# Two passages of a three-stage graph kernel: weights on another queue, columns reloaded in pieces, a pipelined split, and no barrier before the attention

## The reference, cut to what matters

```python
deg = maximum(segment_sum(1, dst), 1);  norm = deg ** -0.5
h = maximum(layernorm(x), 0)
for W_r, W_sl, W_el in (layer 1, layer 2):                 # "messages"
    own = where(in_degree == 0, h @ W_el, h @ W_sl)
    agg = segment_sum((rel_embed[type] + h[src]) @ W_r, dst)
    h = rrelu(agg * norm + own)
x = x + h
h = maximum(layernorm(x), 0)                               # "attention"
qk = h @ Wqk + bqk;  v = h @ Wv + bv
scores = clip(sum(qk[dst] * qk[src], -1) / sqrt(128), -5, 5)
out = segment_sum(softmax over each dst (scores) * v[src], dst) @ Wo + bo
x = x + layernorm(h + out) * gamma + beta
```

## Time and profile before

| | before |
|---|---|
| median of 3 runs | 870.51 us (868.87 to 872.46) |
| the profiled execution's own time | 870.01 us |
| its span, first to last instruction | 868.3 us |
| TensorE busy | 732.6 us, 84% |
| VectorE / ScalarE / GpSimd busy | 61% / 50% / 28% |
| mean granted clock of TensorE | 0.944 of full speed |
| stages by TensorE | counting and layer one to 372.7, passage to 431.2, layer two to 562.4, passage to 573.8, attention to the end |

### The profile page before, as it was taken

How to read it: one execution, slowest core, us unless ns; L and a number is a source line. 1 busy time by engine, 2 the same in 40 slices (tenths; PEclk the granted TensorE clock), 3 DMA queues, 4 the chain that set the end, 5 groups by cost and what they waited for, 6 DMA issues and landing times. The chain is left out here.

```text
span 868.3 us, 15380 instructions
## 1 busy us (share of the span) xinstructions
PE 732.6 (84%) x5767; PEld 545.2 (63%) x5767; DVE 527.7 (61%) x931; ACT 431.5 (50%) x1085; POOL 245.1 (28%) x273
## 2 busy tenths in 40 slices
PE   4266698898889898977399999859999999999993
PEld 3255587788778788866289999824444444444463
DVE  4987997786768677541033333414476767666676
ACT  0445765564555555551011111237767676767661
POOL 6130010000001111100000000026666666666662
PEclk9999799799989999987699999979999999999996
DMA  4100200033300000011311111130000000000000
GB/s 130 33 1 18 59 2 7 23 103 71 100 9 7 8 8 7 8 60 61 108 31 37 36 37 37 37 106 1 1 4 21 3 22 2 24 0 24 2 25 18
DMA packets 39763, 27.89 MB, mean 32 GB/s; under 512 B 5311, under 2 KB 38163, under 8 KB 39686
## 3 DMA queue, kind: packets, MB, share of 16 engines
q1 hardware_dynamic: 39206, 26.35, 10.5%
q10 hardware_dynamic: 480, 0.53, 0.2%
HBM read 13.28 MB, written 10.80 MB: 28 GB/s over the span
## 5 line engine op out<-in xcount | busy, mean ns | idle before, releaser
L1462 POOL TENSOR_TENSOR counts<-counts,work 125x500 f32<-125x500 f32 x150 | 162.3, 1082 | 97.5 <-DVE work L1526 84.1
L1016 PE MATMUL sums<-work 125*128 125x196 f16 (+15 forms) x1220 | 157.1, 256 | 24.7 <-DVE work L825 24.6
L1384 PE MATMUL a_ps_o<-work 125*128 125x500 f32 (+1 forms) x350 | 159.2, 545 | 7.1 <-DVE work L1530 6.7
L1526 DVE SCALAR_TENSOR_TENSOR work<-a_ps_s,counts 125x500 f32<-125x500 f32 x150 | 101.6, 677 | 93.5 <-ACT a_ps_s L1482 93.4
L1372 PE MATMUL a_ps_s<-work 128*125 128x500 f32 x300 | 152.0, 589 | 6.9 <-PEq L534 6.9
L819 DVE TENSOR_TENSOR work<-work,counts 125x3024 f16<-125x3024 f16 (+1 forms) x60 | 114.3, 1906 | 65.5 <-PE sums L1018 62.4
L1477 ACT ACTIVATE a_ps_s<-a_ps_s,work 125x500 f32<-125x500 f32 (+1 forms) x157 | 102.1, 650 | 86.5 <-PE a_ps_s L1372 83.4
L1018 PE MATMUL sums<-work 125*128 125x10 f16 (+15 forms) x800 | 133.7, 196 | 0.0
L1187 ACT CAST counts<-sums 128x364 f32 (+38 forms) x305 | 131.9, 472 | 2.1 <-issue 1.4
L977 PE MATMUL sums<-counts 125*128 125x250 f16 (+1 forms) x975 | 124.5, 275 | 10.0 <-ACT work L1129 10.0
L825 DVE TENSOR_TENSOR work<-work,counts 125x4200 f16<-125x4200 f16 (+15 forms) x120 | 125.5, 1086 | 0.0
(11 more groups left out here) (178 smaller groups left out, 703.3 us busy)
## 6 DMA issues: line engine op xcount, KB each, us to landing
first_columns<-counts SPq DMA_DIRECT2D x5, 610.4 KB
counts<-first_columns SPq DMA_DIRECT2D x5, 610.4 KB
counts<-counts SPq DMA_DIRECT2D x5, 468.8 KB
counts<-in_x SPq DMA_DIRECT2D x5, 312.5 KB
h_nodes<-counts SPq DMA_DIRECT2D x5, 312.5 KB
work<-in_x SPq DMA_DIRECT2D x12, 125.0 KB
x_after_messages<-work SPq DMA_DIRECT2D x12, 125.0 KB
h_attention<-work SPq DMA_DIRECT2D x12, 125.0 KB
```

The source lines that it names most:

```text
L1016: pe.matmul(win[:, 0:c, cols], lo[:, k * 2 * LO:k * 2 * LO + 128], m[:, k, h0 * w:(h0 + c) * w].rearrange("p (h d) -> p h d", d=w), start= ...
L1384: last = pe.matmul(ps_o[c % 2][:, 0:cols(u) // n], h3[:, j + i, :], pbuf[u % PB][:, i * NP:i * NP + cols(u) // n], start=j + i == 0, stop= ...
L1462: pool.tensor_tensor(a, a, p, ALU.add).then_inc(acc_done, 1)
L1526: dve.scalar_tensor_tensor(pbuf[u % PB], ps_s[u % 4][0:NP, 0:WIDE], float(np.exp(-CLIP)), counts[0:NP, j, c * WIDE:(c + 1) * WIDE], ALU.ma ...
```

## The change

Five edits. (1) Layer two's weights and the last chunk's x are issued by ScalarE, after its last split piece. (2) The five DMAs of `first_columns` are issued by SP one per chunk, behind the h3 store of the first five chunks of layer two. (3) h of layer one comes back from the moment at which all batches but the last are free. (4) Between the layers TensorE's steps stand in an order written out; chunk 11 uses other PSUM banks (2 and 3) and another buffer for the turned h; the split is pipelined over pieces on ScalarE and VectorE, and ten source blocks of layer two's first sum stand ahead of agg of chunk 12. (5) The two blocks of engine programs become one: each engine goes from the messages to the attention by itself, the first three scores, two clips, one exponent and one product stand before the last chunk is turned, and that turn and its qk stand inside units 1 and 3.

```diff
 @block.sync
-            sp.wait_ge(ring_free, len(BATCHES))
+            sp.wait_ge(ring_free, len(BATCHES) - 1)
             sp.wait_ge(h1_out, 16 * DIRECT)
...
-            sp.wait_ge(sums_done, CHUNKS)
-            for i in range(5):
-                v = slice(5 * i, 5 * i + 5)
-                sp.dma_start(counts[0:NP, v, 0:HEAD], heads.rearrange("p (j d) -> p j d", d=HEAD)[:, v, :]).then_inc(heads_in, 16)
...
-            for t, v in zip((wr, ws[:, 0:D], ws[:, D:]), weights2):
-                sp.dma_start(t, v).then_inc(L["wts"], 16)
-            sp.dma_start(wqk, wqk_d).then_inc(L["wts"], 16)
-            sp.dma_start(bqk, bqk_d.rearrange("(p o) -> p o", o=1)).then_inc(L["wts"], 16)
-            sp.dma_start(x_last, by_block(x, LAST)).then_inc(L["last_in"], 16)
...
                 sp.dma_start(h3[:, c * LB * D:(c + 1) * LB * D], xc.rearrange("p b f -> p (b f)")).then_inc(L["h3_out"], 16)
+                if i < 5:
+                    v = slice(5 * i, 5 * i + 5)
+                    sp.dma_start(counts[0:NP, v, 0:HEAD], heads.rearrange("p (j d) -> p j d", d=HEAD)[:, v, :]).then_inc(heads_in, 16)
...
             sp.wait_ge(L["x2_last"], 16)
+            sp.wait_ge(L["rows"], CHUNKS)
+            A["sync"](sp)
 @block.vector
             ending(DIRECT)
+            split(0, 0)
             for i in range(4):
-                split(i)
-            split(4)
+                split(i + 1, 0)
+                split(i, 1)
+            split(4, 1)
             ending(DIRECT + 1)
...
                 dve.tensor_scalar(mv2[:, 0:nb, 1], mv2[:, 0:nb, 1], EPS, None, ALU.add).then_inc(L["var"], 1)
+                if i == LAST:
+                    A["vector_first"](dve)
                 dve.wait_ge(L["root"], i + 1)
 @block.tensor
-                    pe.wait_ge(put, 2 * READY[c])
+                    pe.wait_ge(put, 2 * READY[c] if c <= DIRECT else 2 * GROUPS)
...
+            for kind, c in (("own", DIRECT + 1), ("agg", DIRECT), ("sum", DIRECT + 1), ("self", DIRECT + 1),
+                            ("rest", DIRECT + 1), ("own", LAST), ("agg", DIRECT + 1), ("sum", LAST), ("self", LAST), ("rest", LAST)):
+                for step in by_kind.pop((kind, c)):
+                    layer1(*step)
+            own(0, ORDER2[0])
+            sums(0, ORDER2[0], 0, EARLY).then_inc(early, 1)
+            layer1("agg", LAST, 0)
...
-            h3_turn(LAST, ORDER2[LAST])
-            qk(LAST, ORDER2[LAST])
+            pe.wait_ge(L["rows"], LAST)
+            A["tensor_first"](pe)
+            A["tensor"](pe, last_turn, last_qk)
 @block.scalar
+            layer1("own", DIRECT + 1)
+            split(0, 0)
+            for i in range(4):
+                split(i + 1, 0)
+                split(i, 1)
+            split(4, 1)
+            layer1("self", DIRECT + 1)
+            layer1("rest", DIRECT + 1)
+            layer1("own", LAST)
+            split(5, 0)
+            split(5, 1)
+            layer1("self", LAST)
+            layer1("rest", LAST)
+            split(6, 0)
+            split(6, 1)
...
+            act.wait_ge(agg_done, CHUNKS)
+            for t, v in zip((wr, ws[:, 0:D], ws[:, D:]), weights2):
+                act.dma_start(t, v).then_inc(L["wts"], 16)
+            act.dma_start(wqk, wqk_d).then_inc(L["wts"], 16)
+            act.dma_start(bqk, bqk_d.rearrange("(p o) -> p o", o=1)).then_inc(L["wts"], 16)
+            act.dma_start(x_last, by_block(x, LAST)).then_inc(L["last_in"], 16)
...
+            A["scalar_first"](act)
             act.wait_ge(L["x2_ready"], CHUNKS)
             act.dma_start(by_block(x2, LAST), tmp[:, 0:1, :]).then_inc(L["x2_last"], 16)
...
+            A["scalar"](act, last_turned, last_rows)
 def attention
-    with nc.Block() as block:
+    def scalar_first(act):
+        act.wait_ge(consts, 2)
+        below(act, 0)
+        below(act, 1)
+        exponent(act, 0)
+
+    def run_scalar(act, last_turned, last_rows):
+        for u, (c, j, n) in enumerate(units):
+            if 0 < u < len(units) - 1:
+                below(act, u + 1)
+            if u:
+                exponent(act, u)
+            if u == 1:
+                last_turned()
+            if u == 3:
+                last_rows()
```

More of the change, by code:

```diff
@@ L326, in messages @@
     hn_in = [sem(f"hn_in{i}") for i in range(4)]
-    rounded2, parts2_ready = sem("rounded2"), sem("parts2_ready")
+    rounded2, parts2_ready = ([sem(f"{n}{i}") for i in range(2)] for n in ("rounded2_", "parts2_ready"))
+    early = sem("early")
     slots, at_slot = plan()
@@ L458, in again_dve @@
     def again_dve(dve):
+        dve.wait_ge(early, 1)
         dve.memset(zeros_r, 0.0).then_inc(R["begin"], 1)
@@ L528, in messages @@
                                      "h3_t_out", "qk", "power")}
+    L["rows"] = T["rows"]
     LAST = CHUNKS - 1
@@ L1034, in _ @@
                         pe.reg_load(flag, T["flag"][0:1, 0:1])
-            for step in slots[GROUPS]:
-                layer1(*step)
-            with pe.If_ne(flag, 0):
-                again_pe(pe)
             def own(i, c):
@@ L1206, in split @@
                     act.wait_ge(y_done, DIRECT + i - 3)
-                act.copy(parts[:, v, 0, :], hn_n[:, v, :]).then_inc(rounded2, 1)
-                act.wait_ge(parts2_ready, 2 * i + 1)
-                act.copy(parts[:, v, 1, :], hn_n[:, v, :]).then_inc(rounded2, 1)
-            for kind, q, _ in slots[GROUPS]:
-                if kind in ("own", "self", "rest"):
-                    layer1(kind, q)
-                    if kind == "own" and q == DIRECT + 1:
-                        for i in range(5):
-                            split(i)
-                    if kind == "rest" and q == DIRECT + 2:
-                        split(5)
-            split(6)
+                act.copy(parts[:, v, s, :], hn_n[:, v, :]).then_inc(rounded2[s], 1)
+            layer1("own", DIRECT + 1)
[7 more added lines that the diff above has]
+            layer1("own", LAST)
+            split(5, 0)
+            split(5, 1)
+            layer1("self", LAST)
+            layer1("rest", LAST)
+            split(6, 0)
+            split(6, 1)
             flag = act.alloc_register("again_act")
@@ L1616, in attention, with run_sync @@
-    local.close()
+    def run_sync(sp):
+        for s, v in ((wv_s, wv), (wo_s, wo), (bv_c, bv.rearrange("(p o) -> p o", o=1)), (bo_b, bc(bo)), (gamma_b, bc(gamma)), (beta_b, bc(beta))):
+            sp.dma_start(s, v).then_inc(loaded, 16)
+        for c in range(FULL + 1):
+            for h, n in halves(c):
+                if c:
+                    sp.wait_ge(y_ready[h], c)
+                sp.dma_start(xr[h][:, 0:n, :], rows(x2, c, h, n)).then_inc(xr_in[h], 16)
+            for h, n in halves(c):
+                sp.wait_ge(y_ready[h], c + 1)
+                sp.dma_start(rows(out, c, h, n), y[h][:, 0:n, :]).then_inc(y_out[h], 16)
+        sp.wait_ge(y_out[0], 16 * (FULL + 1))
+        sp.wait_ge(y_out[1], 16 * FULL)
@@ new lines, in score @@
+    def score(pe, u):
+        c, j, n = units[u]
+        if u == NB - 1:
+            pe.wait_ge(T["rows"], -(-NB // 2))
+        out = ps_s[u % 4]
+        if c < FULL:
+            last = pe.matmul(out[0:NP, :WIDE], qk_t[:, j * NP:(j + 1) * NP], qk_t[:, c * WIDE:(c + 1) * WIDE], start=True, stop=True)
+        else:
+            for i in range(n):
+                last = pe.matmul(out[0:NP, i * NP:(i + 1) * NP], qk_t[:, (j + i) * NP:(j + i + 1) * NP], qk_t[:, FULL * WIDE:], start=True, stop=True)
+        last.then_inc(scores, 1)
@@ new lines, in below, with exponent @@
+    def below(act, u):
+        act.wait_ge(scores, u + 1)
+        s = ps_s[u % 4][0:NP, 0:cols(u)]
+        act.activation(s, s, ACT.Relu, bias=five, scale=-float(D) ** -0.5).then_inc(limited, 1)
+    def exponent(act, u):
+        act.wait_ge(limited, u + 1)
+        s = ps_s[u % 4][0:NP, 0:cols(u)]
+        act.activation(s, s, ACT.Exp, bias=five, scale=-1.0).then_inc(exped, 1)
+    def scalar_first(act):
[3 more added lines that the diff above has]
+        exponent(act, 0)
@@ new lines, in run_scalar, with take @@
+    def run_scalar(act, last_turned, last_rows):
+        def take(c):
+            act.wait_ge(pv_done, end_unit(c))
+            if c:
+                act.wait_ge(f_done, c)
+            w = blocks(c) * NP
+            act.copy(hv[:, 0:w], ps_o[c % 2][:, 0:w]).then_inc(hv_out, 1)
+        for u, (c, j, n) in enumerate(units):
+            if 0 < u < len(units) - 1:
+                below(act, u + 1)
+            if u:
+                exponent(act, u)
+            if u == 1:
+                last_turned()
+            if u == 3:
+                last_rows()
+            if c == 0 and j == 14:
+                act.wait_ge(wv_turned, 1)
+                act.copy(wv_t, ps_f[:, 0:D]).then_inc(wv_t_out, 1)
+            if c == 0 and j == 17:
+                act.wait_ge(wvo_done, 1)
+                act.copy(wvo, ps_f[:, D:2 * D]).then_inc(wvo_out, 1)
+                act.copy(bvo, ps_f[0:NP, 2 * D:3 * D]).then_inc(wvo_out, 1)
```

(3 more changed lines are left out.)

562 lines of the change are left out of this document (272 added, 290 removed).

## The result

The changed kernel takes 843.76 us (median of 4 runs, 840.8 to 846.48); the kernel before took 870.06 us beside it (868.87 to 872.46). The ratio is 0.969, 95% interval 0.965 to 0.973. The profiled execution took 846.48 us with a span of 844.7, 23.6 less than the span before.

The account below looks back on a forecast made before the run. TensorE, busy 84% of the span, was taken as the bound, losing time to idles and low clock in two passages. 870.0 less 25.2 (first passage) less 5.0 (second) gave 839.8, predicted as 840, range 833 to 848.

Parts of the forecast that it names:

- the prediction's own signs: Column DMAs 11 us apart with no turn wait on VectorE; wrong if layer two takes longer between first and last `weigh`.
- Arrival of TensorE: TensorE reaches layer two's first `weigh` at 404.6 instead of 416.1: 6.7 us from idles, 4.8 from clock.
- The exposed branch: Between the layers, the branch to the second path, hidden under 3.8 us before, now costs 0.2 us.
- The weights: Layer two's first `weigh` starts at 407.2 instead of 431.2, when `bqk` lands; first passage gains 25.2 us with clock.
- The columns in pieces: In layer two each saved-column piece makes x at most a microsecond late; about 5 us are slack, so cost 0.
- the columns only move their price: Layer two: pieces delay x, TensorE waits; fully 31.5 us, 871 (chance 0.02); up to half, 848 to 856 (0.05).
- Start of the attention: From last `rows` to unit 4's product: 6.1 us gained at full clock, 5.0 after 1.1 lost to clock.
- The piece of h3: The attention's first product waits for h3's first piece, landing at 568.8; TensorE idles 2.3 us before unit 0.
- the two stumbles: ScalarE waits for the last turn, then for qk; TensorE idles 2.1 and 1.8 us in units 2 and 4.

## Why the prediction was right, and where it was not

840 was predicted and 843.76 measured, inside 833 to 848; 26.3 us of the 30 forecast came. That is closer than its terms were, and in part luck: without the loss in layer two the kernel would have taken about 832 (843.76 less 11.9, an estimate), below the range. Two of the prediction's own signs went against it. The column DMAs stood 13.5 to 13.9 us apart in place of 11, with waits on VectorE at the turn, and layer two took longer than before between its first and last `weigh`, 138.8 us against 129.9, which it had named as a case of being wrong.

- **Arrival of TensorE (404.6 predicted).** Its sums ended at 405.55. The idle in front of own was 2.74 (2.8 predicted), that in front of agg 11 was 0.62 (0.8). The exposed branch was under-sized: 0.2 was taken, 1.35 us and a second stop of 0.45 measured, both put down to "issue".
- **The weights (407.2).** `weigh` started at 405.87, and it was ScalarE's copy behind the table load that ended the wait (406.1 predicted for it), not a DMA. `bqk` landed in 2.1 us, where 3.6 was taken for its many small rows. The clock hardly fell there, which gave some 1.6 us more. The term was 25.2 (its clock part, 2.9 less 1.6, is 1.3 and was added as 1.2) and is 28.2 up to the second chunk's weigh. There was no drain behind the table load: the copy begins within 0.01 us of its end, so the row of 1.28 us was the better price. The Trainium skill (ScalarE: Activation LUTs, "What ACT_TABLE_LOAD costs") has 2.66 us with a drain that this trace does not show.
- **The queue against the place.** The text credits both the new queue and the moved columns. The experiments separate them: either alone frees the weights; with the columns moved the queue adds nothing; with the queue alone the first x is held in their place.
- **The columns in pieces (0 predicted): the step that failed.** It said that x "comes at most a microsecond late" and that "about 5 us are slack". Both rest on the 5.8 us between the first h3 store and the next x. A round later these are 4.4 us (451.48 to 455.85). And x waits for the landing of that store, which the prediction left out. Put together from rows, the loop without a piece is 3.45 (store), 3.3 (x) and 3.3 us (layer norm), some 10.0 against TensorE's 10.9: the slack was about 1 us a round (an estimate, with the store's landing taken from the changed kernel). With a piece just ahead, x landed 3.4 to 3.9 us later, the loop took 13.5 us, and after two chunks TensorE paid. The price was 11.9 us. It is the rival "the columns only move their price", 38% of its full 31.5 us; that case, up to half of the price, was given a chance of 0.05, too little, for its test was made on one chunk in place of the loop.
- **Start of the attention (5.0).** 7.2 came. The piece of h3 was waited for 1.89 us (2.3 predicted), the two stumbles, the idles in units 2 and 4, were 1.50 and 1.44 (2.1 and 1.8), and the clock held. The mechanism was right and the size off by 2.2: 1.1 for a fall of the clock that did not come, and 1.0 in the stumbles.

So two terms came out 5.2 us better together and one 11.9 worse, which partly cancelled: of 30.2 us added up, 23.6 came between the two traces.

## What to carry to other kernels

A large DMA that is taken off one wait and cut into pieces must be followed round the loop it lands in: add store landing, the piece, the next load and the work behind it, and compare the sum with the period of the bound engine; slack in one round says nothing when the next load waits for the last store. Here the same transfers right behind the small load that was needed soonest cost 10 us less than right ahead of it. And where an engine waits for another's answer inside a pipelined loop, give the answer a few units of distance: here no cost of it showed, and it returned 3.5 us.

## What was not expected of the hardware

The branch around the second path, which these inputs never enter, is followed by a stop of TensorE of 1.3 to 1.8 us in all eleven traces with the changed order, and ten of them have a second stop of 0.2 to 0.9 us some 24 matmuls later. Whether this is the fetch of instructions was not tried. The weight vector of 0.5 KB, the last weight issued, took longer to land beside the columns than the 64 KB matrices ahead of it (6.3 against 3.0 to 4.3 us). In the changed kernel, with no column transfer beside them, it took 2.1 against their 2.4 to 2.5, so its shape alone is not the reason. And the granted clock stayed at its upper level after idles of 2.73 and 3.14 us in one trace and fell after the first of these in the ten others; only several traces tell what such an idle costs.
